# Loads in another order, and the weight fold ahead of the turning, at the beginning of a decoder layer

## The reference

```python
xn = layernorm(x)                                   # no gain, no bias
Q, K, V = xn @ Wq.T, xn @ Wk.T, xn @ Wv.T           # 16 heads of 16
g = clip(sigmoid(xn_heads @ gw.T), 1e-6)            # one gate a head
log_c = clip(cumsum(log(g)), -30, 30)
Gc = exp(log_c) + 1e-6
R = silu(K @ sw.T)
S = cumsum(K x V * R / Gc) * Gc
x = x + einsum(Q, S) @ Wo.T
x = x + mlstm(layernorm(x), ctx, ctx, rpe[hops], ...)
x = x + experts(layernorm(x))
```

## Time and profile before

| | us |
|---|---|
| median of 3 runs | 833.77 |
| the three runs | 833.7, 833.77, 839.5 |
| the profiled execution | 837.07 |
| its span, first to last instruction | 835.2 |
| TensorE busy in the span | 752.2 (90%) |
| VectorE, ScalarE, GpSimd busy | 404.5, 361.6, 433.1 |
| mean granted TensorE clock | 0.966 |

### The profile page before, as it was taken

One profiled execution on the slowest core, in us unless ns is written; L12 is line 12 of the kernel. 1 busy time (PEld: TensorE's weight loads), 2 busy tenths in 40 slices (PEclk: granted clock), 3 DMA queues, 4 the chain that ended last, 5 costly groups with the idle time before them and its releaser, 6 DMA issues.

```text
span 835.2 us, 17124 instructions
## 1 busy us (share of the span) xinstructions
PE 752.2 (90%) x5854; PEld 669.5 (80%) x5855; DVE 404.5 (48%) x1018; ACT 361.6 (43%) x936; POOL 433.1 (52%) x504
## 2 busy tenths in 40 slices
PE   7898888878988889898887889799999999999995
PEld 4666666657978889888877777599999999999995
DVE  2456655555544433332379999723333333333331
ACT  1333333324635433332568764544444444444441
POOL 6566666655676666656446642124444444444442
PEclk8999999998989998998989999999999999999999
DMA  8233333333232335237367799622222222222221
GB/s 291 80 91 107 109 114 112 109 111 95 81 92 82 90 92 186 85 87 189 81 165 223 215 251 329 229 71 38 38 38 35 35 37 38 31 38 38 38 37 20
DMA packets 75813, 88.30 MB, mean 106 GB/s; under 512 B 11952, under 2 KB 66032, under 8 KB 75632
## 3 DMA queue, kind: packets, MB, share of 16 engines
q0 software_dynamic: 19824, 43.93, 21.1%
q1 hardware_dynamic: 52256, 40.11, 16.4%
q10 hardware_dynamic: 3680, 3.54, 1.2%
HBM read 75.82 MB, written 11.73 MB: 105 GB/s over the span
## 4 chain that ended last, share of the span: by engine, by line
PE 40%; issue 27%; POOL 15%; DVE 10%; ACT 5%; another core or an unknown queue 2%; DMA 1%; POOLq 1%; DVEq 0%; ACTq 0%
PE ps L2011 15%; POOL out L1664 8%; PE ps L1031 7%; POOL G L1643 5%; PE ps L485 3%; PE ps L552 2%; PE ps L526 2%; PE ps L478 2%; ACT G L1354 2%; DMA out<-G,slots 1%; DVE U L810 1%; PE ps L450 1%; ACT G L1355 1%; PE ps L1228 1%
## 5 line engine op out<-in xcount | busy, mean ns | idle before, releaser
L332 POOL DMA_INDIRECT G<-in_rpe,hopi x193 | 185.6, 962 | 113.2 <-issue 40.8
L1781 ACT ACTIVATE G<-ps,U 128x128 f32<-128x128 f32 x312 | 84.9, 383 | 162.1 <-PE ps L1717 158.0
L1717 PEld LDWEIGHTS ps<-G,QT 128*128 128x128 f32 x1248 | 146.9, 194 | 2.0
L1717 PE MATMUL ps<-G,QT 128*128 128x128 f32 x1248 | 147.2, 277 | 0.0
L1725 PE MATMUL ps<-G 128*128 x624 | 141.2, 379 | 1.2 <-DVE G L1947 1.2
L1725 PEld LDWEIGHTS ps<-G 128*128 128x128 f32 x624 | 115.5, 190 | 15.7 <-issue 1.6
L2011 PE MATMUL ps<-U,PET 128*128 128x128 f32 (+3 forms) x768 | 106.3, 281 | 9.7 <-issue 9.5
L2011 PEld LDWEIGHTS ps<-U,PET 128*128 128x128 f32 x768 | 98.7, 198 | 12.1 <-issue 11.7
L979 DVE COPY PET<-ps 128x512 f32<-128x512 f32 x64 | 44.0, 689 | 115.0 <-PE ps L1031 79.7
L1664 POOL DMA_INDIRECT out<-G,slots x39 | 69.3, 1776 | 23.6 <-issue 23.6
L2054 ACT ACTIVATE PET<-ps 128x512 f32<-128x512 f32 (+1 forms) x63 | 37.3, 592 | 96.6 <-PE ps L1031 70.1
(11 more groups left out here) (239 smaller groups left out, 1254.1 us busy)
## 6 DMA issues: line engine op xcount, KB each, us to landing
G<-run_max SPq DMA_DIRECT2D x16, 512.0 KB, 6.3
U<-in_w SPq DMA_DIRECT2D x16, 512.0 KB, 7.3
G<-in_w SPq DMA_DIRECT2D x8, 1024.0 KB, 10.5
G<-in_rpe,hopi POOLq DMA_INDIRECT x193
U<-in_ctx SPq DMA_DIRECT2D x8, 256.0 KB
tokens_kept<-X SPq DMA_DIRECT2D x8, 256.0 KB
X<-tokens_kept SPq DMA_DIRECT2D x1, 2048.0 KB
hidden_rows<-QT ACTq DMA_DIRECT2D x8, 256.0 KB, 7.4
```

What stands on the lines that cost most here:

```text
L332: pool.indirect_dma_start(out=dst, out_offset=None, in_=rpe_d, in_offset=bass.IndirectOffsetOnAxis(ap=hopi[:, n:n + 1], axis=0)) \
L1717: mm = pe.matmul(bank(1 + 2 * u + c // 4, 4, P)[:, c % 4], w1c[u][:, k, c], hT[u][:, k, :], start=(k == 0), stop=(k == KC - 1))
L1781: ins = nc.scalar.activation(gel[u][:, c, :], bank(1 + 2 * u + c // 4, 4, P)[:, c % 4], ACT.Gelu, bias=b1c[u][:, c:c + 1])
```

## The change

The constants are laid out anew, so that the identity and the small masks come first, and are loaded in three pieces (identity and masks; the triangular, ones and block masks; the rest). SyncE issues the tokens of sequence 0 first, then the first piece of the constants, the hop indices, the second piece, the tokens of sequence 1, `wg6`, `gbias` and the first context. The tokens of sequences 2 and 3 follow when the first keys are there, with `lnbb` and the last piece; those of sequence b + 3 in iteration b. The two small columns move to the head of ScalarE's queue. TensorE folds the weights ahead of turning the first tokens, one leading `keep_going` of 256 columns goes, the one of 256 columns behind the fold goes too, its wait stands behind the other, and the one ahead of the first scores gets 512 columns. The statistics and the inverse deviation of sequence 1 move behind the fold and between the value copies. The waits follow the loads (`ld_tri`, `ld_g` at 48, `ld_xr` counted, `ld_lnb` at 32).

```diff
--- before.py
+++ after.py
@@ -26,10 +26,9 @@
 MLSTM_EPS = 1e-6
 
 
-C_ID, C_TRI, C_TRIREV, C_ONE, C_BLK = 0, 128, 256, 384, 512
-C_HM16, C_HM32, C_IOTA = 640, 648, 652
-C_TOK, C_RESET, C_PAR, C_CENT, C_PAD = 660, 692, 828, 830, 958
-C_POS, C_SLOT, C_HIGH, C_W = 960, 1088, 1127, 1166
+C_ID, C_HM16, C_HM32, C_PAR, C_TRI, C_TRIREV, C_ONE, C_BLK = 0, 128, 136, 140, 144, 272, 400, 528
+C_IOTA, C_TOK, C_RESET, C_CENT, C_PAD = 656, 664, 696, 832, 960
+C_POS, C_SLOT, C_HIGH, C_W = 962, 1090, 1129, 1168
 HIGH = 1.5 * 2.0 ** 30
 
 
@@ -252,7 +251,7 @@
         kept_dram = nc.dram_tensor("tokens_kept", [NKEPT * P, D], F32).ap().rearrange("(t p) d -> p t d", p=P)
         ld_idx, ld_cst, ld_x, ld_xr = sem("ld_idx"), sem("ld_cst"), sem("ld_x"), sem("ld_xr")
         ld_wv, ld_wq, ld_wkT, ld_wo, zeros = sem("ld_wv"), sem("ld_wq"), sem("ld_wkT"), sem("ld_wo"), sem("zeros")
-        ld_wk, ld_s, ld_g = sem("ld_wk"), sem("ld_s"), sem("ld_g")
+        ld_wk, ld_s, ld_g, ld_tri = sem("ld_wk"), sem("ld_s"), sem("ld_g"), sem("ld_tri")
         w_ready, w_full = sem("w_ready"), sem("w_full")
         ch_v, ch_a = sem("ch_v"), sem("ch_a")
         stage[0] = early
@@ -334,19 +333,31 @@
                 .then_inc(landed, 16)
 
         def tokens_sync(sp):
+            def tokens(b0, b1, landed):
+                sp.dma_start(X[:, 2 * b0:2 * b1], x_d[b0:b1].rearrange("b (c p) d -> p (b c) d", p=P)).then_inc(landed, 16)
+
+            def constants_of(c0, c1, landed):
+                sp.dma_start(cst[:, c0:c1], cst_d[:, c0:c1]).then_inc(landed, 16)
+
+            tokens(0, 1, ld_x)
+            constants_of(C_ID, C_TRI, ld_cst)
             sp.dma_start(hopi[:, :], idx_d).then_inc(ld_idx, 16)
-            sp.dma_start(X[:, 0:4], x_d[0:2].rearrange("b (c p) d -> p (b c) d", p=P)).then_inc(ld_x, 16)
-            sp.dma_start(cst[:, :], cst_d).then_inc(ld_cst, 16)
-            sp.dma_start(gwc, gw_d).then_inc(ld_s, 16)
-            sp.dma_start(swc, sw_d).then_inc(ld_s, 16)
+            constants_of(C_TRI, C_IOTA, ld_tri)
+            tokens(1, 2, ld_g)
             sp.dma_start(wg6, wg_d.rearrange("(k p) n -> p k n", p=P)).then_inc(ld_g, 16)
             sp.dma_start(gbias, gb_d.partition_broadcast(P)).then_inc(ld_g, 16)
-            sp.dma_start(lnbb, lnb_d.partition_broadcast(P)).then_inc(ld_lnb, 16)
-            sp.dma_start(X[:, 4:T], x_d[2:B].rearrange("b (c p) d -> p (b c) d", p=P)).then_inc(ld_xr, 16)
             for b in range(B):
                 if b >= 1:
                     sp.wait_ge(qt_full, b)
                 sp.dma_start(cx, ctx_d[b].rearrange("(c p) d -> p c d", p=P)).then_inc(cx_ld, 16)
+                if b == 0:
+                    sp.wait_ge(k_full, 1)
+                    tokens(2, 4, ld_xr)
+                    sp.dma_start(lnbb, lnb_d.partition_broadcast(P)).then_inc(ld_lnb, 16)
+                    constants_of(C_IOTA, C_W, ld_lnb)
+                elif b + 3 < B:
+                    sp.wait_ge(ld_xr, 16 * b)
+                    tokens(b + 3, b + 4, ld_xr)
                 if b >= 1:
                     sp.wait_ge(x_fin, b)
                     if b >= 2:
@@ -430,9 +441,8 @@
             nil = v2[0].rearrange("p h e -> p (h e)")
 
             pe.wait_ge(zeros, 1)
-            for n in (512, 512, 512, 256):
+            for n in (512, 512, 512):
                 keep_going(n, nil, 6)
-            pe.wait_ge(ld_cst, 16)
 
             def fold_weights():
                 pe.wait_ge(ld_wk, 16)
@@ -442,7 +452,6 @@
                         mm = pe.matmul(bank(0, 512)[:, k * HA + o * HC:k * HA + (o + 1) * HC],
                                        wkN[:, o, k * P:(k + 1) * P], swb, start=True, stop=True)
                 mm.then_inc(w_full, 1)
-                pe.wait_ge(w_ready, 2)
 
             def turn(dst, src, done):
                 for k in range(KC):
@@ -509,6 +518,8 @@
             def cum(b):
                 pe.wait_ge(lg_r, b + 1)
                 pe.wait_ge(kk_r, b + 1)
+                if b == 0:
+                    pe.wait_ge(ld_tri, 16)
                 o = bank(7, 2, NRC, HA)
                 pe.matmul(o, tri, lgg[b % 2].unsqueeze(2).to_broadcast([P, 2, NRC, HA]), start=True, stop=False)
                 pe.matmul(o[:, 1], ones, lgg[b % 2][:, 0:1, :].to_broadcast([P, NRC, HA]), start=False, stop=True) \
@@ -599,12 +610,14 @@
 
             for b in range(-1, B + 1):
                 new, now, old = b + 1 < B, 0 <= b < B, b >= 1
+                if b < 0:
+                    fold_weights()
+                    pe.wait_ge(ld_cst, 16)
                 if new:
                     tokens_turned(b + 1)
                 if b < 0:
                     keep_going(256, nil, 6)
-                    fold_weights()
-                    keep_going(256, nil, 6)
+                    pe.wait_ge(w_ready, 2)
                 if now and b >= 1:
                     score(b, 0)
                 if new:
@@ -639,7 +652,7 @@
                 if new:
                     key(b + 1)
                 if b < 0:
-                    keep_going(256, nil, 6)
+                    keep_going(512, nil, 6)
                     score(0, 0)
                 if old:
                     queries_turned(b - 1)
@@ -659,6 +672,8 @@
 
         def tokens_scalar(act):
 
+            act.dma_start(gwc, gw_d).then_inc(ld_s, 16)
+            act.dma_start(swc, sw_d).then_inc(ld_s, 16)
             act.dma_start(wkN, wk_d.rearrange("(k p) n -> p k n", p=P)).then_inc(ld_wk, 16)
             act.dma_start(wvx[:, :, 0:D], wvT_d.rearrange("(k p) n -> p k n", p=P)).then_inc(ld_wv, 16)
             act.dma_start(wqT, wqT_d.rearrange("(k p) n -> p k n", p=P)).then_inc(ld_wq, 16)
@@ -714,7 +729,6 @@
                 nc.scalar.activation(lgg[b % 2], coef[b % 2], ACT.Ln).then_inc(lg_r, 1)
 
             inv_std(rstd[0], mv[0][:, :, 1], mv_r, 1, rstd_r)
-            inv_std(rstd[1], mv[1][:, :, 1], mv_r, 2, rstd_r)
             for b in range(-1, B + 1):
                 new, now, old = b + 1 < B, 0 <= b < B, b >= 1
                 if new:
@@ -723,6 +737,8 @@
                     expand_gates(b)
                 if new:
                     values(b + 1, 0)
+                if b < 0:
+                    inv_std(rstd[1], mv[1][:, :, 1], mv_r, 2, rstd_r)
                 if old:
                     if b >= 2:
                         act.wait_ge(gate_full, b - 1)
@@ -871,18 +887,18 @@
 
             nc.vector.memset(v2[1], 0.0)
             dve.wait_ge(ld_x, 16)
-            for b in range(2):
-                stats(b, st[b], mv[b], mv_r)
-            norm(0, xna, mv[0], rstd[0], rstd_r, xn_r)
+            stats(0, st[0], mv[0], mv_r)
             dve.wait_ge(ld_cst, 16)
             dve.wait_ge(ld_s, 32)
             nc.vector.tensor_scalar(swb, hm16, swc, None, ALU.mult).then_inc(w_ready, 1)
             dve.wait_ge(ch_v, 1)
             for k in range(KC):
                 nc.vector.tensor_scalar(wvx[:, k, D + k * HC:D + (k + 1) * HC], hm16, gwc, None, ALU.mult)
+            norm(0, xna, mv[0], rstd[0], rstd_r, xn_r)
             dve.wait_ge(w_full, 1)
             nc.vector.tensor_copy(wvx[:, :, D + HA:D + 2 * HA], bank(0, KC, HA)).then_inc(w_ready, 1)
-            dve.wait_ge(ld_g, 32)
+            dve.wait_ge(ld_g, 48)
+            stats(1, st[1], mv[1], mv_r)
             nc.vector.tensor_tensor(wg6[:, 2:4, :], wg6[:, 2:4, :], wg6[:, 4:6, :], ALU.add).then_inc(w_ready, 1)
             for b in range(-1, B + 1):
                 new, now, old = b + 1 < B, 0 <= b < B, b >= 1
@@ -913,8 +929,7 @@
                 if new:
                     sigmoids(b + 1)
                 if 0 <= b and b + 2 < B:
-                    if b == 0:
-                        dve.wait_ge(ld_xr, 16)
+                    dve.wait_ge(ld_xr, 16 * max(b, 1))
                     stats(b + 2, st[b % 2], mv[b % 2], mv_r)
                 if b + 2 < B:
                     dve.wait_ge(xt_full, b + 2)
@@ -929,7 +944,7 @@
                     clamp(gc[(b + 1) % 2], bank(7, 2, NRC, HA)[:, :, 0, :], cum_full, b + 2, cl_r)
                 if old:
                     if b == 1:
-                        dve.wait_ge(ld_lnb, 16)
+                        dve.wait_ge(ld_lnb, 32)
                     add_lnb(b - 1)
```

## The result

| | before | changed |
|---|---|---|
| median of 7 runs each, one chip, us | 833.7 | 837.08 |
| lowest and highest | 830.49, 839.5 | 834.5, 839.41 |
| ratio of the times | | 1.0059, 95% interval 1.0034 to 1.0084 |
| profiled execution, us | 837.07 | 834.5 |
| its span | 835.2 | 832.7 |

The changed kernel is slower by 0.6%, 3.4 us. The pair shows where time goes in the beginning; what the two spans differ by is no result.

A forecast was written before the change was run, and what follows sets the result against it. TensorE, busy 752.2 of 835.2 us, was taken as the bound, with loads a bottleneck only at the beginning. 3.6 us off the start, nothing given back, from 833.77 gave 830.2 us; range 826 to 834.5, likeliest 829 to 831.5.

The forecast's parts named there:

- Tokens at 4.1, dummies' end at 6.79 as the new gate, fold behind them: Kernel start: tokens land at 4.1 instead of 6.39; TensorE's dummies, ending at 6.79, gate the fold instead.
- rival (b): ScalarE's queue: small packets delay Wk, fold up to 1.3 us later, 831.5; or sequence 1's loads late, 832; shared chance 0.25.
- First projection at 10.3: TensorE's first projection, after fold, turning and dummy, begins at about 10.3 instead of 13.90, gaining 3.6 us.
- Rival (a): TensorE's start: full clock from the fold on shortens the stretch by another 3.0 us, 827.2 at the end; chance 0.2.
- Second sequence's statistics: VectorE, behind the fold: moving them costs nothing, provided their three loads land by about 13.5; expected 10 to 11.
- Longer dummy: Ahead of the first scores: 256 more columns, 0.43 us, hidden by ScalarE's copy of the keys, so no cost.
- tokens a sequence ahead: Later sequences' token loads: issued about a sequence, some 20 us, before their statistics, so they cost nothing.
- Gathers: GpSimd's start: begins at about 5.1 instead of 3.60, catches up within two or three sequences; cost nothing, otherwise 1.5 us.
- The sum: Whole kernel: 3.6 us off the start, nothing given back, 830.2 us against 833.77, 0.4% less.
- (d): From 20 to 40 us: TensorE stays at half speed after the fold; 5.4 us longer, 839; chance 0.07 including further dips.
- (c): Later stages: shifted lulls change clock dips, 1.8 us either way, 828.4 or 832.0, two more 833.8; shared chance 0.25.
- Rival (e): Whole kernel: no change, 833 to 834.5, the start's gain being waited for later; shared chance 0.25.

The follow-up runs named there:

- e1_again: Changed kernel as it is, run again in a faster series: 776.69 us, one run, against a median of 779.75 for the kernel before.
- e9_changed_third: Changed kernel as it is, timed on another chip in a slower series: 835.83 us (5 runs), ratio to before 1.0054.
- e6_changed_timed: Changed kernel as it is, with more runs in a faster series: 776.15 us (12 runs) against 778.16, ratio 0.9981.
- e8_old_loads: Changed kernel with all loads back in old order and queues, fold still ahead of turning; faster series: 780.87 us, ratio to before 1.004.
- e4_dummy256: Changed kernel with the dummy ahead of the first scores back from 512 to 256 columns; faster series: 775.74 us, one run.
- e2_upfront: Changed kernel, tokens of sequences 2 and 3, lnbb and last constants not waiting for first keys; faster series: 775.44 us, ratio to before 0.9962.
- e3_later: Changed kernel, loads behind the first keys waiting for the first cumulative sums instead; faster series: 775.97 us, ratio to before 0.997.
- e14_idx_first: Changed kernel with the hop indices first on SyncE's queue, ahead of the first tokens; slower series: 832.28 us against 832.32, ratio 1.0001.
- e11_late_gathers: Changed kernel with all position-row gathers put behind GpSimd's list for the sequences, first at 142 us; slower series: 956.4 us, one run.
- e13_five_ahead: Changed kernel with five gathers issued ahead instead of ten, the other five at the list's end; slower series: 835.78 us, ratio to before 1.0038.
- e10_lead4: Changed kernel with its fourth leading dummy of 256 columns back; slower series: 838.96 us (4 runs), ratio to before 1.0099.
- e7_turn_first: Changed kernel with TensorE's old order, turning ahead of fold and four leading dummies, new loads kept; faster series: 772.52 us, ratio to before 0.9933.
- e5_before_again: Kernel before as it is, run again for a trace in a faster series: 780.57 us, one run.

## Why the prediction was wrong, step by step

The time, 837.08, lies outside the range of 826 to 834.5 and on the other side of 833.77, though within 1%.

- **Tokens at 4.1, dummies' end at 6.79 as the new gate, fold behind them: right in the profiled run.** 4.04, 6.83 and no gap. (In other runs Wk was the gate, see rival (b).)
- **First projection at 10.3: too late by 0.8.** It came at 9.49, since the fold took 1.25 us to the next matmul instead of 1.85, and what follows ran at full clock (turning 0.63, dummy 0.60). Rival (a)'s mechanism was true at the start: the two halves of the values took 1.21 and 1.24 us instead of 2.13 and 1.55. First scores at 20.34 rather than 20.9. From first projection to first scores it still took 10.9 us (10.6 before), since the keys' completion was held for 2.0; in the free `e1_again` it took 9.0, with first scores at 18.26. The first mask is 5.5 ahead in free runs.
- **Second sequence's statistics: right.** They begin at 11.94 (13.5 was the limit).
- **Rival (b), the queue of ScalarE: its term was real and counted little.** Wk took 4.8 us from its issue instead of the 3.3 of the earlier trace rows. Landings in the DMA view of the changed kernel (queue, KB, us from issue to landing):

```profile
X<-in_x SPq DMA_DIRECT2D x2, 256.0 KB, 3.3
U<-in_wk ACTq DMA_DIRECT2D x1, 256.0 KB, 4.8
...
hopi<-in_idx SPq DMA_DIRECT2D x1, 128.5 KB, 4.7
```

It was in at 6.5, just ahead of the dummies' end. Where these ended sooner, it was the gate: in `e9_changed_third` they end at 6.29 and the fold starts at 6.40; in the free `e6_changed_timed` they end at 5.98, and TensorE stands idle for 0.66 until Wk is in and the fold starts at 6.63. The Trainium skill ("DMA: Bandwidth & Descriptors", section "Queues, rings and completion order") has each DMA engine take turns between queues a packet at a time; tokens in 3.3 us and Wk in 4.8 agree with that rule. In `e8_old_loads`, with the small packets and all other loads back in their old places, Wk took 3.5. No run put the small packets elsewhere with the rest unchanged, so it isn't shown that they are the cause.

- **Longer dummy, tokens a sequence ahead: right.** `e4_dummy256`, `e2_upfront` and `e3_later` moved the first mask by 0.1 to 0.6 us.
- **Gathers, "Cost nothing; 1.5 us if it were never made up": this step failed.** It failed twice. Its size: the indices landed after 4.7 us, not about 3.3, and GpSimd began at 6.78 rather than 5.1, 3.2 us later than in the earlier trace rows. Its question: I asked who reads the gathered rows (nobody before 205 us) and how long GpSimd needs to catch up. I didn't ask what else waits while it catches up. In before the unbroken row ends at 18.59, behind which GpSimd waits twice for TensorE (from 18.59 and from 20.46), and the copy of the second value half comes 1.1 us late (matmuls' end 18.22, copy 19.29). With the start 3.2 later and TensorE 4 us earlier, GpSimd never has to wait for TensorE's signals and runs without a break to 25.57, right over the first scores. In held runs the keys' completion is seen 2.0 us late within that row, and that of the scores only 2.5 us behind its end. What I expected to be slack was a row of work that held up the others' signals.
- **The sum.** Forecast: 3.6 off, nothing back. Held: 4.2 off up to the first scores, 6.7 back from there to the first mask (5.7 of it TensorE standing still), another 1.5 with half speed up to 38.5 us (4.0 behind at the mask of sequence 1), and 3.4 and 4.4 slower at the medians of the two comparisons. `e14_idx_first` takes the loss to nothing with one line moved; in `e11_late_gathers` no completion is late until the first gather. `e13_five_ahead` warns against reading the loss as the hole alone: without the hole it was still 0.4% slower.
- **Rivals (c) and (d).** (d) had the right picture, TensorE at half speed behind the first sequence's preparation (21.4 to 38.5), for a wrong reason: the fold took 1.40 us instead of 1.85, turning and projections ran at the full clock, and it fell at 21.4, behind the idle 1.87 us ahead of the scores. In `e9_changed_third`, with the first scores at the same time, it fell at 25.9, within the long standstill. (c) was at work in free runs: 5.5 us of lead at sequence 7 turned into 2.0 at the medians, with half-speed stretches between 205 and 560 us.
- **Rival (e).** "Nothing seems to wait for an absolute time except DMA" was the wrong sentence: in `e9_changed_third` and `e10_lead4` the scores' semaphore rises at 28.08 whether TensorE comes 0.7 us earlier or later. The end of GpSimd's row is such a time (25.56 in both), set by when the indices land.
- **A flaw in the reading of before.** Its trace had held completions: releases "remote" behind idle times of 1.4 to 3.5 us, as quoted above. Had I looked for these, the gathers would have been the first suspect. Rival (a) took one of them for slow work: of the 2.4 us that it counts for the second value half (16.88 to 19.29) the last 1.1 are the late completion.

What stays open: why the runs of one series are held and those of another free, with the same kernels; what in a gather holds TensorE's completions, or whether the matmuls themselves end late, which modelled ends can't tell; what lets one through within a row and another only behind it; where the lead of `e13_five_ahead` goes; and whether `e7_turn_first`'s gain in free runs is more than the fall of the lulls.

## What to carry to other kernels

A queue of work that "has slack" because nobody reads its results soon may still be in the way of others: before a load is moved behind others, ask how the engine that it starts behaves against the rest (here an unbroken row of gathers, whose end moved from 18.59 to 25.57) and not only when its results are read. A release that the profile calls "remote", or an instruction that begins microseconds after the end of all it needs, is worth following before anything is predicted. And a change of half a per cent is to be measured on more than one chip: this one is 0.6% slower in held runs, and in free ones 0.2% quicker or the same.

## What the runs showed of the hardware that I had not expected

- The same kernel takes 778 to 780 us in some series and 831 to 836 in others, at nearly the same mean granted clock (0.979 in `e5_before_again`, 0.966 in the trace of before). The difference lies where position rows are gathered: from the end of the last such gather on both take 430 us (405.6 to 835.2, 348.8 to 778.8), and from the first expert on 279.
- In the slower series TensorE's completions come late while GpSimd gathers without a pause: 3.2 us in before (91.28 to 94.52), 6.6 us in the changed kernel (21.49 to 28.11), over 11 us in `e11_late_gathers`, and none there up to the first gather at 142 us.
